# Two of eight pairs of gathers without their addition, and the addition moved to the vector engine

## The reference

```python
q = (x @ Wq + bq).reshape(n, H, C)
k = (x @ Wk + bk).reshape(n, H, C)
v = (x @ Wv + bv).reshape(n, H, C)
e = (edge_attr @ We + be).reshape(-1, H, C)
k_j = k[src] + e
q_i = q[dst]
alpha = jnp.einsum('ehc,ehc->eh', q_i, k_j) / sqrt(C)
# softmax of alpha over the edges of one dst -> alpha
msg = (v[src] + e) * alpha[..., None]
out = jax.ops.segment_sum(msg, dst, num_segments=n)
```

## Time and profile before

| | us |
|---|---|
| three runs | 4489.6, 4495.13, 4501.59 (median 4495.13) |
| the profiled execution | 4536.35 |
| its span | 4534.3 |
| POOL busy | 2747.6 |
| DVE busy | 2841.2 |
| PE busy | 3193.4 |
| ACT busy | 2087.4 |

### The profile page before, as it was taken

The page is one execution under the profiler, slowest core; times in us unless marked ns, Lnnn a source line. Parts: engine busy times, 40 slices in busy tenths (PEclk is TensorE's granted clock), DMA queues, the critical chain, the costliest instruction groups (busy, mean ns, idle before and its releaser), DMA issues. The chain is left out here.

```text
span 4534.3 us, 53017 instructions
## 1 busy us (share of the span) xinstructions
PE 3193.4 (70%) x11623; PEld 2184.1 (48%) x11623; DVE 2841.2 (63%) x7130; ACT 2087.4 (46%) x6027; POOL 2747.6 (61%) x2215
## 2 busy tenths in 40 slices
PE   4555553466666763777775778888887878888884
PEld 3444442244444442444443356666664456666662
DVE  3445447344444455666666568888887578888887
ACT  3344444011111221322233258877875167788785
POOL 4666662666666003766661088888883188888881
PEclk7766776687888875656666889999998999999997
DMA  4544443466656303444432399999995599999993
GB/s 134 109 113 112 111 112 78 151 186 188 197 184 182 101 18 103 113 112 113 111 107 42 129 195 188 194 189 190 190 188 113 161 191 189 194 187 191 193 181 90
DMA packets 378980, 661.07 MB, mean 146 GB/s; under 512 B 59011, under 2 KB 161396, under 8 KB 378677
## 3 DMA queue, kind: packets, MB, share of 16 engines
q0 software_dynamic: 190208, 406.78, 47.1%
q1 hardware_dynamic: 184356, 247.08, 17.2%
q10 hardware_dynamic: 4112, 3.83, 0.3%
HBM read 582.15 MB, written 75.33 MB: 145 GB/s over the span
## 5 line engine op out<-in xcount | busy, mean ns | idle before, releaser
L1653 POOL DMA_INDIRECT t_kv<-kv_tab,srcT x880 | 1411.1, 1604 | 636.8 <-ACT t_kv L1770 378.4
L1280 POOL DMA_INDIRECT grow<-h_tab,srcT x440 | 449.2, 1021 | 478.3 <-POOLq L83 279.0
L776 POOL DMA_INDIRECT grow<-x_tab,srcT x440 | 444.4, 1010 | 310.0 <-issue 109.6
L1841 PE MATMUL bank<-t_kv,t_oh 128*128 128x260 f32 x1760 | 534.9, 418 | 97.1 <-ACT t_oh L1781 54.9
L476 POOL DMA_INDIRECT grow<-h_tab,srcT x440 | 437.3, 994 | 253.2 <-issue 99.0
L1813 PE MATMUL bank<-we,t_aT 128*128 128x256 f32 x1760 | 517.6, 421 | 25.9 <-DMA t_aT<-attrT_tab 25.5
L1824 PE MATMUL bank<-H,t_ohT 128*128 x1760 | 502.2, 412 | 20.3 <-DVE t_ks L1684 19.9
L1800 ACT ACTIVATE t_kv<-t_kv 128x64 f32<-128x64 f32 x1760 | 461.6, 333 | 0.7 <-DVE t_kv L1700 0.6
L824 DVE TENSOR_TENSOR acc<-acc,bank 128x272 f32 x440 | 192.5, 438 | 405.8 <-PE bank L901 157.9
L1724 DVE TENSOR_TENSOR acc<-acc,bank 128x260 f32 x880 | 369.0, 419 | 106.4 <-DVE acc L1724 72.3
L1841 PEld LDWEIGHTS bank<-t_kv,t_oh 128*128 128x128 f32 x1760 | 304.0, 198 | 264.9 <-ACT t_oh L1781 100.2
(11 more groups left out here) (397 smaller groups left out, 5139.2 us busy)
## 6 DMA issues: line engine op xcount, KB each, us to landing
t_aT<-attrT_tab SPq DMA_DIRECT2D x110, 512.0 KB
lob<-lo_tab SPq DMA_DIRECT2D x110, 256.0 KB
arow<-in_edge_attr SPq DMA_DIRECT2D x440, 64.0 KB
attrT_tab<-aT SPq DMA_DIRECT2D x55, 512.0 KB
t_lob<-lo_tab SPq DMA_DIRECT2D x110, 256.0 KB
grow<-h_tab,srcT POOLq DMA_INDIRECT x880
t_kv<-kv_tab,srcT POOLq DMA_INDIRECT x880
kv_tab<-kv SPq DMA_DIRECT2D x10, 1290.0 KB, 5.2
```

What stands on the lines that cost most here:

```text
L776: nc.gpsimd.indirect_dma_start(out=grow[:, t % RA, 0:F], out_offset=None, in_=x_tab, in_offset=bass.IndirectOffsetOnAxis(ap=srcT[:, t:t + ...
L1280: nc.gpsimd.indirect_dma_start(out=grow[:, t % R2, :], out_offset=None, in_=h2_tab, in_offset=bass.IndirectOffsetOnAxis(ap=srcT[:, t:t + 1 ...
L1653: nc.gpsimd.indirect_dma_start(out=kv[:, t % UB, :], out_offset=None, in_=kv_tab, in_offset=bass.IndirectOffsetOnAxis(ap=srcT[:, t:t + 1], ...
L1841: nc.tensor.matmul(PS[4 + t % WIN3][:, 0:LHW], oh[:, t // HB % 2, t % HB, :], kv[:, t % UB, F:KVW], start=True, stop=True).then_inc(produc ...
```

## The change

In steps 4 and 6 of a round the pair becomes "plain". POOL gathers its two tiles without adding, and waits only until the ring's place is free (`products`), not for ACT. ACT no longer fills it. PE makes its edge terms not six steps but one step ahead, right before the queries of that pair, so the order in which pairs use the two banks is a new list (`edge_order`; `place[p]` is a pair's place in it). DVE adds the edge terms from PSUM to the k part and to the v part before it multiplies by the queries, and its signal `v_added` frees the bank. SP, DVE's weighing and ACT's weighing wait by the new order. The diff (some lines that only follow from it are left out):

```diff
+        def plain(p):
+            return p % 8 in (4, 6)
+        def edge_order():
+            order = [p for p in range(AHEAD + 1) if not plain(p)]
+            for p in range(ET // 2):
+                order += [n for n in (p + AHEAD + 1,) if n < ET // 2 and not plain(n)]
+                order += [n for n in (p + 1,) if n < ET // 2 and plain(n)]
+            return order, {p: j for j, p in enumerate(order)}
...
@@ gpsimd
+                            if plain(p):
+                                if t % 2 == 0 and t >= UB:
+                                    pool.wait_ge(products, t + 2 - UB)
+                                nc.gpsimd.indirect_dma_start(out=kv[:, u, :], out_offset=None, in_=kv_tab, in_offset=row).then_inc(g_ready[u], 16)
+                            else:
+                                if t % 2 == 0:
+                                    pool.wait_ge(filled, p + 1 - plains(p))
+                                nc.gpsimd.indirect_dma_start(..., compute_op=ALU.add).then_inc(g_ready[u], 16)
@@ sync
-                                sp.wait_ge(e_ready, 4 * (g - 2))
+                                sp.wait_ge(e_ready, max(place[p] for p in range(4 * (g - 3), 4 * (g - 2))) + 1)
@@ vector
+                        def add_edge_terms(p):
+                            s = 2 * p % UB
+                            e = PS[place[p] % 2][:, :].rearrange("p (v f) -> p v f", v=2)
+                            dve.wait_ge(e_ready, place[p] + 1)
+                            for v in range(2):
+                                dve.wait_ge(g_ready[s + v], gathered(2 * p + v, UB))
+                            nc.vector.tensor_tensor(kv[:, s:s + 2, 0:F], kv[:, s:s + 2, 0:F], e, ALU.add).then_inc(k_added, 1)
+                            part = u_rows[:, s:s + 2, :, 0:C3]
+                            nc.vector.tensor_tensor(part, part, e.rearrange("p v (h c) -> p v h c", h=H3), ALU.add).then_inc(v_added, 1)
+                            dve.wait_ge(k_added, plains(p) + 1)
...
                             if p < pairs:
+                                if plain(p):
+                                    add_edge_terms(p)
                                 times_q(p)
@@ scalar
-                            if p + AHEAD < pairs:
+                            if p + AHEAD < pairs and not plain(p + AHEAD):
                                 fill(p + AHEAD)
@@ tensor, edge_terms
-                            if p >= 2:
-                                pe.wait_ge(filled, p - 1)
+                            if j >= 2:
+                                last = edge_pairs[j - 2]
+                                if plain(last):
+                                    pe.wait_ge(v_added, plains(last) + 1)
+                                else:
+                                    pe.wait_ge(filled, last + 1 - plains(last))
...
-                            if p + AHEAD + 1 < pairs:
+                            if p + AHEAD + 1 < pairs and not plain(p + AHEAD + 1):
                                 edge_terms(p + AHEAD + 1)
+                            if p + 1 < pairs and plain(p + 1):
+                                edge_terms(p + 1)
```

More of the change, by code:

```diff
@@ L1627, in graph_layers, with plains @@
         WIN3 = 3
+        def plain(p):
+            return p % 8 in (4, 6)
+        def plains(p):
+            return sum(plain(i) for i in range(p))
+        def edge_order():
[4 more added lines that the diff above has]
+            return order, {p: j for j, p in enumerate(order)}
         def attend(layer):
             tag = f"t{layer}"
-            names = "lo_in0 lo_in1 lo_in2 at_in0 at_in1 at_in2 oht_ready oh_ready e_ready filled q_ready q_used sums_done msg_ready act_ready products added zeroed dve act".split()
+            names = "lo_in0 lo_in1 lo_in2 at_in0 at_in1 at_in2 oht_ready oh_ready e_ready filled q_ready q_used sums_done msg_ready act_ready products added zeroed k_added v_added dve act".split()
             (lo_in0, lo_in1, lo_in2, at_in0, at_in1, at_in2, oht_ready, oh_ready, e_ready, filled, q_ready, q_used, sums_done, msg_ready, act_ready,
-             products, added, zeroed, dv, ac) = [sem(f"{tag}_{n}") for n in names]
+             products, added, zeroed, k_added, v_added, dv, ac) = [sem(f"{tag}_{n}") for n in names]
             lo_in, at_in = (lo_in0, lo_in1, lo_in2), (at_in0, at_in1, at_in2)
@@ L1637, in attend @@
             STEPS = pairs + LAG + 1
+            edge_pairs, place = edge_order()
             with ExitStack() as scope:
@@ L1650, in _ @@
                         for t in range(ET):
[L1651 to L1655, removed]
+                            p, u = t // 2, t % UB
+                            row = bass.IndirectOffsetOnAxis(ap=srcT[:, t:t + 1], axis=0)
+                            if plain(p):
[5 more added lines that the diff above has]
+                                    pool.wait_ge(filled, p + 1 - plains(p))
+                                nc.gpsimd.indirect_dma_start(out=kv[:, u, :], out_offset=None, in_=kv_tab, in_offset=row, compute_op=ALU.add).then_inc(g_ready[u], 16)
                     @block.sync
@@ L1764, in fill @@
                             u = 2 * p % UB
-                            e = PS[p % 2][:, :].rearrange("p (v f) -> p v f", v=2)
-                            act.wait_ge(e_ready, p + 1)
+                            e = PS[place[p] % 2][:, :].rearrange("p (v f) -> p v f", v=2)
+                            act.wait_ge(e_ready, place[p] + 1)
                             if 2 * p >= UB:
@@ L1784, in _ @@
                         for p in range(AHEAD):
-                            fill(p)
+                            if not plain(p):
+                                fill(p)
                         for p in range(STEPS):
                             b, k, q = p // 8 - 1, p % 8, p - LAG
-                            if p + AHEAD < pairs:
+                            if p + AHEAD < pairs and not plain(p + AHEAD):
                                 fill(p + AHEAD)
@@ L1796, in _ @@
                                     act.wait_ge(sm.w_taken, q // 8 + 1)
+                                    act.wait_ge(v_added, plains(min(pairs, q + 8)))
                                 for t in range(2 * q, 2 * q + 2):
@@ L1829, in _ @@
                         for p in range(AHEAD + 1):
-                            edge_terms(p)
+                            if not plain(p):
+                                edge_terms(p)
                         queries(0, blocks)
```

7 lines of the change are left out of this document (4 added, 3 removed).

## The result

The changed kernel took 4542.14 us in the median against 4498.36 us for the kernel before: a ratio of 1.0094 (95% interval 1.0074 to 1.0113), 44 us slower. The sign was forecast and the time lies in the range (4530 to 4680), but the forecast was +99 us: the size was off by more than a factor of two.

A forecast was written before the change was run, and what follows sets the result against it. Gathers on POOL (30.6 us a round) and DVE were taken as nearly equal bounds. Additions +133, gather waits -24.5 and starts -9.5 gave +99 us on 4495, so 4594 us, range 4530 to 4680.

The forecast's parts named there:

- What bounds the kernel: In `attend`, POOL's back-to-back gathers, 30.6 us a round, and DVE, which waits for them only 0.35 to 0.63 us a round.
- the sum: Both runs of `attend`: additions +133, gather waits gone -24.5, starts -9.5, together +99 us.
- The plain gather's price: On POOL, a gather without addition saves from nothing to 0.594 us; 0.594 taken, 2.38 us a round.
- The new additions: On DVE, two additions per plain pair cost 1.21 to 1.44 us, 1.33 taken; 50 pairs in each of two runs, +133 us.
- The start: First two rounds of each run: DVE waits for gathers, so plain tiles save 4.8 us a run, 9.5 us for both.
- wait for k_added: On DVE, the second addition covers this wait, so nothing; at most 0.42 us a pair.
- Nothing is covered: DVE's wait for PE before pair 4's multiplication hides none of the additions; otherwise at most 1.16 and 0.71 us a round.
- Its own sign of being wrong: In the profile after, DVE's idle time per round shrinking by over 1 us would show the forecast wrong.
- DVE's waits absorb it: Rival: DVE's waits for others, 2.37 and 2.23 us a round, take up the additions; +9, 4504 us; chance 0.09.
- The loop through PE gets longer: Rival: PE's falling clock, just-in-time edge terms and banks freed by DVE add +50 to +100, 4645 to 4695 us; chance 0.18.
- gather-bound rival: Gathers alone set the beat, DVE's idle time takes the additions, 216 plain tiles save 128 us, 4367 us; chance 0.07.
- SP's later loads and the banks freed by DVE: SP's attribute load behind a later e_ready, and PE's banks freed by DVE instead of ACT, both put at nothing.

The follow-up runs named there:

- e10: Kernel before, with DVE's loads of block numbers into registers moved ahead of the same step's multiplication by the queries; ratio to the kernel before 0.9999.
- e13: Kernel before, with DVE's register loads ahead of the multiplication and PE's step 3 edge terms at the end of step 2; ratio 1.0000.
- e15: Changed kernel, only pair 4 plain but its tiles gathered with addition, DVE's register loads and PE's step 3 edge terms moved earlier; ratio 0.9995.
- e1: Changed kernel without DVE's two additions, so edge terms are missing in pairs 4 and 6; ratio to the kernel before 0.9926, -32 us.
- e5: Kernel before, with two more DVE additions into spare memory ahead of the multiplication of pairs 4 and 6; ratio 1.0221, +96 us.
- e3: Changed kernel with only pair 4 of a round plain, pair 6 as in the kernel before; ratio to the kernel before 1.0065.
- e8: Changed kernel, with DVE's loads of block numbers into registers moved ahead of the same step's multiplication by the queries; ratio to the kernel before 1.0012.
- e7: Changed kernel with one more 512 KB copy in device memory per group of eight tiles, issued by SP; ratio to the kernel before 1.0105.
- e2: Changed kernel with the plain tiles gathered with addition from the ring's second lap on; ratio to the kernel before 1.0105, +46 us.
- e4: Changed kernel with only pair 6 of a round plain; ratio to the kernel before 1.0034.
- run 129: Not a run label: the text reads "the first run", the first of two runs of `attend`, then 129 us, DVE's idle time in the kernel before.
- e12: Changed kernel with only pair 4 plain, DVE's register loads ahead of the multiplication and PE's step 3 edge terms at the end of step 2; ratio 0.9898.
- e11: Changed kernel, with PE making the edge terms of step 3 at the end of step 2, ahead of the scatter; ratio to the kernel before 1.0017.

## Why the prediction was right or wrong

- **What bounds the kernel: right.** Two bounds at nearly the same time. POOL's 30.6 us a round is real (e10, e13 and e15 return to a ratio of 1.000 however much DVE saves), and DVE had 0.35 to 0.63 us to gain from it. e1 measured -32 us, where the sum had 24.5 + 9.5; that the two agree is in part luck, since e1's starts gave 1.5 us and its other idle times moved both ways.
- **The plain gather's price: right.** 0.983 us in the median against 1.541, so the row of 516 floats costs hardly more than that of 258; the addition is what costs.
- **The new additions: 133 us, measured 120.** 0.60 us start to start each, at the low end of 1.20 to 1.44 for the pair. The wait for k_added is free.
- **The start: -9.5 us, measured about -2.5.** The first 16 pairs took 57.8 and 57.4 us, against 59.6 and 58.1. Behind the first multiplication DVE's waits for gathers fell from 20.2 and 20.6 us to 13.2 and 14.1, 13.5 us in all, but the eight pairs of additions there took 8 x 1.2 = 9.6 us back: the prediction had them covered by the waits and counted the saving in full besides.
- **"Nothing is covered": the step that failed.** The sum held every other idle time of DVE fixed. Per round, in the mean of both runs, the idle time before the multiplication and the new additions, mostly waits for PE, fell by 0.34 us beyond the 0.49 for gathers (0.60 in the first run, 0.08 in the second), the idle time at the rescaling by 0.38 and at L1223 by 0.24: 0.96 us, some 48 us over 50 rounds. The prediction reasoned rightly that the order of PE's work gives pair 4's wait no cover, and e5, +96 us, shows that DVE's work by itself makes only the rescaling's idle time give way. But it took the size of the waits as given by the order of work alone. One goes with where PE's half-clock stretch falls (e3), and the other two are mostly register loads (e8) whose length changes with the rest of the program. What shortened them stays open. It is not the DMA traffic (e7), and they stay short with adding gathers (e2); the rescaling's also shrinks with DVE's added work alone (e5) and with the plain gathers alone (e1), and does not in e4. Where a load falls beside the gathers fits these, but was not varied by itself. The prediction had not priced the rescaling's 0.95 us at all, and had L1223's down as a wait for PE. Its own sign of being wrong, DVE's idle time shrinking by over 1 us a round, is there: in the windows of the first run 129 us of 735.9 were idle before and 88 after, 5.4 and 3.8 us a round.
- **The balance:** 99 - 13 (additions) + 7 (start) - 48 (idle times) = +45, against +44 measured in the runs and +38 between the multiplications of the two profiled executions.
- **The rivals.** "DVE's waits absorb it" was nearer than its place in the order: it named the mechanism, idle time of DVE that gives way, though it listed one wait wrongly and missed one. "The loop through PE gets longer" had the sign of the clock wrong here (0.94 to 0.97), but it is what happened in e3's first run. The gather-bound rival is excluded by e1: 32 us of its 128.
- **SP's later loads and the banks freed by DVE** at nothing: nothing in the rows of after speaks against it.

## What to carry to other kernels

Where two engines bound a loop at nearly the same time, relief for one is worth only the other's wait for it, and is paid in full if the relief costs the other one work: here the plain gather was worth nothing beside two plain pairs of additions (e2), and 1% with one plain pair and both moves, which gave DVE room (e12 against e15). Before adding work to an engine, look through all its idle rows: those named "issue" can be register loads, and moving two of these was worth nearly as much as the change cost (e8), though nothing where POOL set the beat (e10). Do not hold an engine's other waits fixed in a sum when the change moves the phase of its neighbours; bound them from below by zero, and from above by more than their present size, since they can grow too (the wait for PE in e1 from 26.4 to 39.8 us).

## What the runs showed of the hardware

- An indirect gather of 128 rows of 516 floats keeps POOL busy for 0.983 us in the median without and 1.541 us with the addition; with rows of 258 floats and no addition it is 0.946 us.
- A register load of eight numbers on DVE took 0.59 us at best and up to 1.5 us in the kernel before, and shows as "issue" idle time of the instruction behind it; moved ahead of the multiplication of its step it left none at L1223 (e8).
- The same instruction form costs DVE 0.60 us when the next one does not have to wait for it and 0.72 us when it does, at a length of 0.68 (L1684 and the new additions); additions on 64 partitions that write bf16 cost 1.33 us a pair instead of 1.20 (e5).
- Of the gathers of the kernel before that began while the multiplication of two SBUF operands (L1708) ran, 44 of 55 took 1.9 to 2.6 us; the 96 that were already running when it began all took 1.54 to 1.56.
- The same code can run in two rhythms in one execution: 31.8 and 30.5 us a round in e3, at a granted clock of 0.91 and 0.95. Four passes placed in an idle stretch of 1.36 us went with a rise of the clock from 0.97 to 0.99 (e11).
- More DMA traffic, 217 instead of 184 GB/s at a DMA share of 0.95, slowed nothing here (e7).
